# Turning a kernel's mixed rows by 16-bit DMA transposes instead of f32 transposes on TensorE

## What is computed

```python
h = _layernorm(x) * (1 + ca) + sa
# mixing: xn = h / norm(h) * sqrt(512) * gamma; q, kv, a = split(xn @ W_qkva.T); a = sigmoid(a)
#   y[t] = a[t] * y[t - 1] + kv[t]        (along the 4096 tokens, for each channel)
x = x + ga * (q * y)
h = _layernorm(x) * (1 + cb) + sb
# FFN: fp4-quantised linear layers, h = silu(gate) * up, then down
x = x + gb * _L0_ffn_ref(h, w_gate, w_up, w_down)
```

## Time and profile before

| | us |
|---|---|
| median of 3 runs (lowest to highest) | 1967.26 (1966.83 to 1967.97) |
| the profiled execution, device time | 1967.09 |
| its span in the profile | 1965.3 |
| granted TensorE clock, mean over the span | 0.997 |
| TensorE busy | 1937.0 |
| VectorE busy | 1688.0 |
| GpSimd busy | 1200.1 |
| ScalarE busy | 629.8 |

### The profile page before, as it was taken

How to read it: one execution, slowest core, us unless ns; L and a number is a source line. 1 busy time by engine, 2 the same in 40 slices (tenths; PEclk the granted TensorE clock), 3 DMA queues, 4 the chain that set the end, 5 groups by cost and what they waited for, 6 DMA issues and landing times.

```text
span 1965.3 us, 27185 instructions
## 1 busy us (share of the span) xinstructions
PE 1937.0 (99%) x9403; PEld 927.9 (47%) x9403; DVE 1688.0 (86%) x2106; ACT 629.8 (32%) x885; POOL 1200.1 (61%) x1072
## 2 busy tenths in 40 slices
PE   7999999999999999999999999999999999999998
PEld 3444444444444444444444444444444444444443
DVE  7786867676869999999999999999999999999985
ACT  4333433433423323233233232323323222332321
POOL 1554765546535776677677667667767766766731
PEclk9999999999999999999999999999999999999999
DMA  8866676657552433433433443343343333334232
GB/s 291 271 182 139 174 169 156 166 152 189 138 116 75 103 73 84 96 72 77 97 78 72 91 90 73 83 99 73 75 96 81 72 89 91 72 80 100 67 75 63
DMA packets 421251, 218.22 MB, mean 111 GB/s; under 512 B 359858, under 2 KB 359870, under 8 KB 421188
## 3 DMA queue, kind: packets, MB, share of 16 engines
q1 hardware_dynamic: 421188, 217.39, 45.2%
HBM read 95.43 MB, written 33.57 MB: 66 GB/s over the span
## 4 chain that ended last, share of the span: by engine, by line
PE 89%; DVE 4%; DMA 2%; POOL 1%; issue 1%; SPq 1%; ACT 1%; DVEq 0%; POOLq 0%
PE bank L1067 44%; PE bank L986 20%; PE bank L1087 15%; PE bank L1091 7%; PE bank L1011 1%; SPq L398 1%; DMA arena<-in_L_attn_x_dram 1%; DVE arena L1291 0%; DVE arena L1162 0%; DVE bn L1151 0%; PE bank L925 0%; PE bank L1102 0%; DMA arena<-in_L_ffn_w_up_dram 0%; POOL arena L568 0%; DMA arena<-arena 0%
## 5 line engine op out<-in xcount | busy, mean ns | idle before, releaser
L1067 PE MATMUL bank<-wgu_hi,arena 128*128 128x512 f16 (+1 forms) x3072 | 870.5, 362 | 2.0 <-DVE arena L1400 2.0
L1067 PE MATMUL bank<-wgu_lo,arena 128*128 128x512 f16 (+1 forms) x1536 | 555.8, 362 | 0.0
L986 PE MATMUL bank<-arena,wq_hi 128*128 128x512 f16 x1536 | 456.9, 379 | 3.4 <-DMA arena<-arena 2.3
L1067 PEld LDWEIGHTS bank<-wgu_hi,arena 128*128 128x128 f16 x3072 | 300.9, 98 | 311.0 <-issue 4.0
L986 PE MATMUL bank<-arena,wq_lo 128*128 128x512 f16 x768 | 291.1, 379 | 0.0
L1087 PE MATMUL bank<-wd_hi,arena 128*128 128x512 f16 x693 | 262.6, 379 | 0.0
L1087 PE MATMUL bank<-wd_lo,arena 128*128 128x512 f16 x693 | 262.6, 379 | 0.0
L986 PEld LDWEIGHTS bank<-arena,wq_hi 128*128 128x128 f16 x1536 | 149.9, 98 | 178.2 <-DMA arena<-arena 2.8
L1067 PEld LDWEIGHTS bank<-wgu_lo,arena 128*128 128x128 f16 x1536 | 150.4, 98 | 154.0 <-issue 0.6
L1400 DVE SCALAR_TENSOR_TENSOR arena<-bank,small,arena 128x512 f32<-128x512 f32 (+1 forms) x192 | 134.1, 700 | 88.6 <-PE bank L1067 82.6
L663 POOL TENSOR_TENSOR arena<-arena 128x512 f32<-128x512 f32 x63 | 153.2, 2432 | 92.4 <-DVE arena L1475 92.4
(11 more groups left out here) (162 smaller groups left out, 2748.2 us busy)
## 6 DMA issues: line engine op xcount, KB each, us to landing
arena<-in_L_attn_x_dram SPq DMA_DIRECT2D x32, 1024.0 KB, 5.9
arena<-x_scratch SPq DMA_DIRECT2D x128, 256.0 KB, 3.2
x_scratch<-arena SPq DMA_DIRECT2D x16, 1024.0 KB, 4.4
out_dram<-arena SPq DMA_DIRECT2D x64, 256.0 KB, 3.1
arena<-in_L_wmod_dram SPq DMA_DIRECT2D x6, 1024.0 KB, 14.2
arena<-arena SPq DMA_TRANSPOSE x258, 3.5
wgu_hi<-in_L_ffn_w_gate_dram SPq DMA_DIRECT2D x1, 2816.0 KB, 12.1
wgu_lo<-in_L_ffn_w_up_dram SPq DMA_DIRECT2D x1, 2816.0 KB, 19.0
```

Source lines behind the costliest of these rows:

```text
L986: last = pe.matmul(dst[m % 2][:, :].rearrange("p (j t) -> p j t", j=NJ), w[:, k, at], uT[p][:, half, :, k, :], start=(n == 0), stop=(n == ...
L1067: last = pe.matmul(dst[n][:, 0:w], xT[p][:, half, k, :], wt[:, k, cut], start=(m == 0), stop=(m == 3 * KD - 1))
```

## The change

TensorE's `turn_mix` goes. VectorE writes the product q * ga * state over the decay buffer of its block, in f32. ScalarE copies that buffer as 16-bit integers into `mix_bits`, the two halves of each f32 number into separate planes (`split_mix`, one instruction of 1024 elements for each m). SyncE turns the planes by DMA, two transposes of 2048 columns for each group: q = 0 for the blocks m = 0 and 1, q = 1 for m = 2 and 3 (`turn_mix(i, q)`, into `mixT_bits`). ScalarE joins the planes again, one instruction of 1024 elements for each token block j, into one of two buffers `mix_rows` (`join_mix`), and VectorE adds from there to `xr`. A join waits until both transposes have landed. The scan keeps two `state` buffers instead of four, and copies its last column to a small `carry` for the next group.

The places: in SyncE's program `turn_mix(i - 1, 1)` stands at the head of group i, `turn_mix(i, 0)` in group i behind `turn_u` and `load_group` and ahead of `weight_turns(i, 1, 3)`. In ScalarE's, `split_mix(i - 1, 3)` stands ahead of decay 0, joins 0 and 1 ahead of squares 0 and 1, `split_mix(i, 0)` and joins 2 and 3 between decay 1 and squares 2 and 3. The store of the last group's x1 moves behind the FFN's slot 0.

```diff
-        mixT, uT = [None, None], [None, None]
-        mixT[0] = view(CH * GT).rearrange("p (c t) -> p c t", c=CH)
+        uT = [None, None]
+        HC = CH // 2
...
+        mix_bits = view(CH * GT).bitcast(U16).rearrange("p (q h j m t) -> p q h j m t", q=2, h=2, j=NJ, m=HC)
         decay = [view(GT) for _ in range(2)]
...
-        mixT[1] = view(CH * GT).rearrange("p (c t) -> p c t", c=CH)
+        mixT_bits = view(NJ * D).bitcast(U16).rearrange("p (q h j c) -> p q h j c", q=2, h=2, j=NJ)
         xr = view(NJ * D).rearrange("p (j d) -> p j d", j=NJ)
...
-        state = [view(GT) for _ in range(CH)]
+        state = [view(GT) for _ in range(2)]
+        mix_rows = [view(D) for _ in range(2)]
...
+                def turn_mix(i, q):
+                    sp.wait_ge(mix_split, CH * i + HC * (q + 1))
+                    wait(sp, mix_joined, NJ * i)
+                    sp.nop(nofuse=True)
+                    sp.dma_start(mixT_bits[:, q].rearrange("p h j (m c) -> p (h j m) c", c=P),
+                                 mix_bits[:, q].rearrange("p h j m t -> p (h j m t)"),
+                                 transpose=True).then_inc(mixT_loaded[q], 16)
...
                         sp.wait_ge(ssq_ready, NJ * NGA)
                         for t in range(2):
                             sp.dma_start(xn_in[t], x1_tile[t]).then_inc(x_in_loaded[t], 16)
+                    if i:
+                        turn_mix(i - 1, 1)
+                    if i == NGA - 1:
                         for t in range(2):
                             load_normalised(t + 2, t)
                     weight_turns(i, -1, 0)
...
                     if 0 < i < NGA - 1:
                         turn_u(i + 1, 1 - p)
                         load_group(i + 3)
+                    turn_mix(i, 0)
                     weight_turns(i, 1, 3)
...
-                sp.wait_ge(x1_ready, NJ * NGA)
-                sp.dma_start(x1_group[NGA - 1], xr).then_inc(x1_stored, 16)
-                sp.wait_ge(x1_stored, 16 * NGA)
+                turn_mix(NGA - 1, 1)
                 for t in range(-1, 3):
                     slot(t, t % 2)
+                    if t == 0:
+                        sp.wait_ge(x1_ready, NJ * NGA)
+                        sp.dma_start(x1_group[NGA - 1], xr).then_inc(x1_stored, 16)
+                sp.wait_ge(x1_stored, 16 * NGA)
...
                 def decays(i, m):
                     act.wait_ge(a_ready, CH * i + m + 1)
-                    wait(act, state_ready, CH * i + m - 1)
+                    wait(act, mix_split, CH * i + m - 1)
                     act.activation(decay[m % 2], a_bank[m % 2][:, :], ACT.Sigmoid,
                                    scale=col("qkva_scale")).then_inc(decay_ready, 1)
+                def split_mix(i, m):
+                    q = m // HC
+                    act.wait_ge(mix_ready, CH * i + m + 1)
+                    wait(act, mixT_loaded[q], 16 * i)
+                    act.activation(mix_bits[:, q, :, :, m % HC, :],
+                                   decay[m % 2].bitcast(U16).rearrange("p (j t h) -> p h j t", j=NJ, h=2),
+                                   ACT.Copy).then_inc(mix_split, 1)
+                def join_mix(i, js):
+                    for q in range(2):
+                        act.wait_ge(mixT_loaded[q], 16 * (i + 1))
+                    for j in js:
+                        wait(act, x1_ready, NJ * i + j - 1)
+                        act.activation(mix_rows[j % 2].bitcast(U16).rearrange("p (q c h) -> p q c h", q=2, h=2),
+                                       mixT_bits[:, :, :, j, :].rearrange("p q h c -> p q c h"),
+                                       ACT.Copy).then_inc(mix_joined, 1)
...
                         squares(1, 1)
+                        split_mix(0, 0)
                         decays(0, 2)
                         u_hi(1, 1)
                         apply(2, 0)
+                        split_mix(0, 1)
                         decays(0, 3)
+                        split_mix(0, 2)
                         return
+                    split_mix(i - 1, 3)
                     decays(i, 0)
+                    if not more:
+                        join_mix(i - 1, (0, 1))
...
                     if more:
+                        join_mix(i - 1, (0, 1))
                         squares(i + 1, 1 - p, (0, 1))
                     decays(i, 1)
+                    split_mix(i, 0)
+                    join_mix(i - 1, (2, 3))
                     if more:
                         squares(i + 1, 1 - p, (2, 3))
...
                     weights(1)
+                    split_mix(i, 1)
                     decays(i, 2)
                     weights(2)
...
                     decays(i, 3)
+                    split_mix(i, 2)
                     if i + 2 < NGA:
                         apply(i + 2, p)
...
                 groups(group)
+                split_mix(NGA - 1, 3)
                 silu(0, 0, 0, 0)
                 steps_of_x(2, 0)
                 silu(0, 0, 0, 1)
                 x_hi(2, 0)
+                join_mix(NGA - 1, (0, 1))
...
                         h_hi(0, 0)
+                        join_mix(NGA - 1, (2, 3))
                         steps_of_x(3, 1)
                         x_hi(3, 1)
...
-                def turn_mix(i, p, js):
-                    for j in js:
-                        if j == 0:
-                            pe.wait_ge(mix_ready, CH * (i + 1))
-                        wait(pe, x1_ready, NJ * i + j - 1)
-                        for m in range(CH):
-                            last = pe.transpose(t_bank[j % 2][:, m * P:(m + 1) * P], mixT[p][:, m, j * P:(j + 1) * P],
-                                                ident[:, :])
-                        last.then_inc(mix_turned, 1)
...
                     product_a(i, p, 0)
                     product_kv(i, p, 0)
                     product_q(i, p, 0)
-                    if i == 1:
-                        pe.wait_ge(mod_copied, NROW)
-                    turn_mix(i - 1, 1 - p, (0, 1))
                     product_a(i, p, 1)
                     product_kv(i, p, 1)
-                    turn_mix(i - 1, 1 - p, (2, 3))
                     product_q(i, p, 1)
...
                 def down(i, p):
-                    if isinstance(i, int) and i == 0:
-                        pe.wait_ge(x1_ready, NJ * NGA)
                     wait(pe, hT_hi_loaded[p], 8 * (i - p) + 16)
...
                 def tile(i, p, b, first, last, b3, b4):
                     gate_up(i, p, 0)
                     if isinstance(i, int) and i == 0:
-                        turn_mix(NGA - 1, 1, (0, 1))
+                        pe.wait_ge(mix_ready, CH * NGA)
                     if not (isinstance(i, int) and (i < 2 or i == LAST)):
                         down(i - 2, p)
                     gate_up(i, p, 1)
-                    if isinstance(i, int) and i == 0:
-                        turn_mix(NGA - 1, 1, (2, 3))
                     gate_up(i, p, 2)
...
+                carry = col("gamma_q", KD)
                 def mix(i, p, b, m, first):
                     dve.wait_ge(decay_ready, CH * i + m + 1)
                     dve.wait_ge(kv_ready, CH * i + m + 1)
-                    dve.tensor_tensor_scan(state[m], decay[m % 2], kv_bank[m % 2][:, :],
-                                           0.0 if first else state[m][:, GT - 1:GT],
+                    if not first:
+                        dve.wait_ge(carry_ready, CH * (i - 1) + m + 1)
+                    dve.tensor_tensor_scan(state[m % 2], decay[m % 2], kv_bank[m % 2][:, :],
+                                           0.0 if first else carry[:, m:m + 1],
                                            ALU.mult, ALU.add).then_inc(state_ready, 1)
                     dve.wait_ge(state_ready, CH * i + m + 1)
+                    dve.tensor_copy(carry[:, m:m + 1], state[m % 2][:, GT - 1:GT]).then_inc(carry_ready, 1)
                     dve.wait_ge(q_ready, CH * i + m + 1)
-                    wait(dve, mix_turned, NJ * (i - 1))
-                    dve.scalar_tensor_tensor(mixT[p][:, m, :], q_bank[m % 2][:, :], ga[:, m, b:b + 1], state[m],
+                    dve.scalar_tensor_tensor(decay[m % 2], q_bank[m % 2][:, :], ga[:, m, b:b + 1], state[m % 2],
                                              ALU.mult, ALU.mult).then_inc(mix_ready, 1)
...
                 def add_x(i, js):
                     for j in js:
                         if j == 0:
                             wait(dve, xr_loaded, 16 * (i + 1))
-                        dve.wait_ge(mix_turned, NJ * i + j + 1)
-                        dve.tensor_tensor(xr[:, j, :], t_bank[j % 2][:, :], xr[:, j, :], ALU.add).then_inc(x1_ready, 1)
+                        dve.wait_ge(mix_joined, NJ * i + j + 1)
+                        dve.tensor_tensor(xr[:, j, :], mix_rows[j % 2], xr[:, j, :], ALU.add).then_inc(x1_ready, 1)
...
                 hidden(0, 0, 0, 0)
-                add_x(NGA - 1, (0, 1))
                 quantise_x(2, 0)
```

(10 more changed lines are left out.)

## The result

| | before | after |
|---|---|---|
| median (lowest to highest), us | 1967.62 (1966.83 to 1968.63) | 2060.79 (2059.17 to 2061.76) |
| profiled execution / its span, us | 1967.09 / 1965.3 | 2061.76 / 2060.0 |
| granted TensorE clock, mean | 0.997 | 0.978 |

The ratio is 1.0475, with a 95% interval of 1.0463 to 1.0488: slower by 93 us, in the direction that was forecast, 37 us beyond the forecast of 2024 and 0.8 us above the range.

A forecast was written before the change was run, and what follows sets the result against it. TensorE bounds the mixing stage at 32.8 us a period; the change makes SyncE's x1 loop bind at 35.4. 1967.1 + 22.0 (start) + 27.4 (steady) + 7.4 (end) = 2024 us, range 1966 to 2060.

The forecast's parts named there:

- D: Time from a group's xr load to the landing of the second turn of mix: 23.4 us, between 21.6 and 25.3.
- term (a): First link of the new period, SyncE's queue from xr load to second mix turn landed: D, 23.4 us of 35.4.
- the start: From the last product of group 0 to xr load 5: load at 262.1 instead of 240.13, +22.0 us.
- the upper one: Upper bound of D, DMA engines as the limit: 18.3 us plus 7.0 for 32 more blocks, 25.3 us.
- The lower sum: Lower bound of D, engines having room: 16.1 to last weight turn, 1.3 issue, 4.2 landing, 21.6 us.
- Term (b): ScalarE's chain in program order: joins 0 and 1, two squares, decay, split 0, joins 2 and 3, 6.75 us.
- copies at double cost: Rival: ScalarE's copies at a 2-byte stride take 1.94 us each, 63 us more, 2087 us; chance 0.06.
- Term (c): Last links of the period: VectorE's last addition and wake-ups, 0.9 us, then x1 store to xr load, 4.33 us.
- Steady: Nine periods, loads 5 to 14, at 35.4 instead of 32.79 us, plus 3.9 for down weights: +27.4 us.
- End: After load 14: group 14's first additions 25.4 instead of 20.9 us behind it, 2.9 more before scan 1: +7.4 us.
- both low bounds: Rival: period 31.8 us with D at 21.6 and cheap copies, about 1974 us; chance 0.05 within 0.2%, 0.07 above.
- Room in the loop: Rival: silent DMA stretch absorbs the turns, TensorE stays the bound and 28 us are gained, 1941 us; chance 0.13.

The follow-up runs named there:

- The late order: Changed kernel with joins, additions, both mix turns, x1 store and xr load moved later on ScalarE, VectorE and SyncE: 1975.82 us, ratio 1.0038.
- copies alone: Kernel before with two scan buffers, the carry and eight ScalarE copies a group of data nobody needs: 1968.80 us, ratio 1.0007.
- Turns alone: Kernel before with two scan buffers, the carry and two 2048-column DMA transposes a group that nobody reads: 1988.57 us, ratio 1.0103.
- another order: Changed kernel with the next weight's raw load issued ahead of turn_mix(i, 0) instead of behind it: 2071.26 us, ratio 1.0524.
- mended order: The late order with FFN's first x1 loads and turn of x(1) earlier, last group's split 3, joins, additions moved: 1960.48 us, ratio 0.9959.

## Why the prediction was right in direction, and wrong in size

**Direction and mechanism held.** TensorE lost 28 us of work and the time rose, because x1 of the group before closes a loop over SyncE's queue, ScalarE and VectorE. The late order, with every turn and copy in it, took 85 of the 93 us away (2060.8 to 1975.8); copies alone cost nothing. Turns alone cost 21 us with no join in the kernel, so a part of the rise needs no loop over the joins; that part the forecast did not have. **Two steps failed:** the size of D in term (a), and in the start the period from load 3 to load 4, which the forecast took for a steady one with 2.5 us added.

**Term (a), D, was mis-sized:** 23.4 us forecast, 25.6 measured. What failed is the choice of the middle between two bounds, for which no row spoke; the upper one, 25.3, was nearly right. The lower sum had links of the right kind, 16.1 + 1.3 + 4.2. Its 1.3 us for the issue of a turn came from the earlier trace rows (512 columns in 1.36 us, 1408 in 1.39); a turn of 2048 columns right behind the 1 MB load took 5.24, and with it this sum, too, is 25.5. The upper bound had the DMA engines as the limit, and they were in fact 0.95 busy over D, with 0.22 us to a block as forecast. So both accounts reach the number. The swap of turn and load, with the same bytes, took 1.5 us off D, so the order has a part in it; how the 2.2 us divide between order and traffic stays open. The 3.3 us that 30 blocks less took off D don't decide it, since another wait, on the raw weight, ended D in that run.

**Term (b), 6.75 us,** measured 7.1 (456.65 to the end of the last join, 463.76). A split took 1.04 us and a join about 1.1, against 0.97: the row of the same element count was the right one to go by, and the rival of copies at double cost falls. **Term (c)** held: addition and wake-ups 0.75, against 0.9, store to load 4.33 as before. From the first join to the next xr load it is 12.2 us, against 12.0.

**The start** was forecast at +22.0 and came to +39.2. Load 2 was late by another 4.7 us (154.62 against 149.9; the two turns of group 0 alone took 10.70 us to issue), the next period by 2.6 us, which is D again, and the period from load 3 to load 4 by 9.7 (47.6 against 37.9). Here the step failed that priced this period at 35.4 and 2.5 us "for weight 3". D alone was 31.05 us in it (192.66 to 223.71) instead of 23.4, because the second turn could not be issued before split 3, at 219.36. The 2.5 us were for turns between mix and the store; from the first join to load 4 it took 16.5 us against 14.5. Split 3 stood behind two chains that reached it within half a microsecond of each other: one from VectorE's wait for the raw weight, 9.68 us, behind the turn of 6.08 us, and one from ScalarE's wait for the turns of the weight, 9.59 us. With the first cut to 5.75 us by another order the period was still 46.6. That both come late because of the turn ahead of them on the queue is a reading of the rows; no run took away both in this period alone.

**Steady:** nine periods of 37.85 us against 35.4, with 3.9 for the down weights: 18 us over, which D's 2.2 us a period account for. **End:** +10.0 against +7.4, not taken apart.

**What the forecast lacked** is the step of the weight that stands ahead of the joins on ScalarE. It waits for two things, the raw weight by way of VectorE and the landing of the weight's turns. In the changed kernel the turns come last, and the step ends about half a microsecond before the second turn of mix lands. With one block in each turn the raw weight came last, and kept D at 22.2 us when the turns cost next to nothing. The D of the rival "both low bounds", 21.6, is about the least that this order gave even then (21.2 to 21.6 us at loads 6 to 9). "Room in the loop" fails in the order of the change, and is what the mended order reaches in its steady groups. Its price for the DMA engines, 27.7 us of work a period, was right: 0.72 of 37.63 us are 27.1.

**The rule on transposing DMAs** (the Trainium skill, Advanced Engine Details and Errata, X-Bar Transpose) that they are as fast as regular ones isn't borne out: a turn of mix, 512 KB, lands in 4.3 us at best, and the store of x1, 1024 KB, in 4.33. By the rule the forecast would have been further off.

## What to carry to other kernels

When work moves from an engine into a queue of DMAs, write down what stands behind it in that queue, raw loads and other turns alike, and follow each to the engine that waits for it and to what waits behind that. A single buffer that is stored, loaded and added to ties three programs together: here it paid to move all three and cost to move one side. If a change removes real work and the time rises, order the loop anew before giving the change up; and look at the last group by itself, where another stage's first loads stand behind the same queue.

## What the runs showed of the hardware

**The issue of a transposing DMA isn't a fixed price.** 2048 columns took 1.68 us at the least, 2.00 ahead of a 1 MB load and 5.24 right behind it.

**A wait costs TensorE more than its length.** After an idle time of 4.9 us the granted clock was 0.57 over six microseconds (441 to 447); two matmuls of 512 columns then took 1.04 us instead of 0.60. Not every wait did this: at 479.31, after 4.15 us, the same pair took 0.60. In the period shown TensorE was busy 32.76 us with work that takes 31.1 a group at the full clock.

**A copy of 1024 16-bit elements at a stride of 4 bytes cost about what 1024 contiguous f32 did:** 1.04 us for a split and 1.16 for a join alone, next to 1.06 for the conversion of 1024 f32 elements to bf16.
